# GNN layer and mixture-of-experts FFN on one core: the first value of four columns per placement tile multiplied by GpSimd instead of VectorE

## The reference

```python
def _L0_gnn_ref(x, W1, b1, W2, b2, edge_index):
    dst = edge_index[0]
    nbr = edge_index[1]
    agg = jax.ops.segment_sum(x[nbr], dst, num_segments=n)
    cnt = jax.ops.segment_sum(jnp.ones((nbr.shape[0],), x.dtype), dst, num_segments=n)
    mean = agg / jnp.maximum(cnt, 1.0)[:, None]
    return x @ W1.T + b1 + mean @ W2.T + b2
...
x = x + _L0_gnn_ref(_layernorm(x, axis=-1), ..., edge_index)
x = x + _L0_ffn_ref(_layernorm(x, axis=-1)[None], ...)[0]
```

## Time and profile before

| | us |
|---|---|
| Median of 3 runs | 1964.03 |
| Lowest and highest of them | 1962.31, 2257.03 |
| The profiled execution's own time | 1958.99 |
| Span in its trace | 1956.9 |
| Placement of the first group in it (first L1472 to last L1486 on VectorE) | 68.41 to 104.84 |
| First gather (L650) | 108.33 |

### The profile page before, as it was taken

How to read it: one execution, slowest core, us unless ns; L and a number is a source line. 1 busy time by engine, 2 the same in 40 slices (tenths; PEclk the granted TensorE clock), 3 DMA queues, 4 the chain that set the end, 5 groups by cost and what they waited for, 6 DMA issues and landing times.

```text
span 1956.9 us, 41490 instructions
## 1 busy us (share of the span) xinstructions
PE 1768.8 (90%) x11167; PEld 1495.9 (76%) x11167; DVE 967.5 (49%) x2315; ACT 1117.8 (57%) x3316; POOL 1193.3 (61%) x1141
## 2 busy tenths in 40 slices
PE   6888998899887898878877879999999999999997
PEld 4655875588555677656665768999999999999997
DVE  6868977898467787633334786311111111111111
ACT  5964875477544699755652657544444444444443
POOL 1167777788777777777777743444554454544543
PEclk9989999999999899999999989999999999999999
DMA  9333333333333333344443767724424424242421
GB/s 313 101 88 103 95 98 102 101 90 86 100 104 103 100 97 95 104 127 139 144 138 110 243 229 236 222 36 128 125 40 121 98 66 120 39 127 38 124 36 20
DMA packets 113112, 224.31 MB, mean 115 GB/s; under 512 B 27286, under 2 KB 76604, under 8 KB 107094
## 3 DMA queue, kind: packets, MB, share of 16 engines
q0 software_dynamic: 61152, 129.45, 26.7%
q1 hardware_dynamic: 32576, 74.98, 11.2%
q10 hardware_dynamic: 19254, 18.32, 3.0%
HBM read 371.77 MB, written 34.91 MB: 208 GB/s over the span
## 4 chain that ended last, share of the span: by engine, by line
PE 46%; POOL 31%; issue 11%; DMA 6%; DVE 4%; SPq 1%; ACT 1%; DVEq 0%; POOLq 0%; ACTq 0%
POOL arena L650 31%; PE bank L1315 19%; PE bank L1331 18%; DMA arena<-ytab,arena 4%; PE bank L1280 2%; PE bank L1055 2%; PE bank L1101 1%; PE bank L1303 1%; DMA gw<-in_gw2t 1%; SPq L465 1%; DVE agg L1949 1%; DMA ytab<-arena 1%; DMA agg<-in_b 0%; DMA agg<-xtab_a,arena 0%; PE bank L1255 0%
## 5 line engine op out<-in xcount | busy, mean ns | idle before, releaser
L650 POOL DMA_INDIRECT arena<-ytab,arena x784 | 800.6, 1021 | 240.1 <-issue 230.9
L1280 PE MATMUL bank<-arena 128*128 x2356 | 631.4, 395 | 111.4 <-SPq L525 109.9
L1280 PEld LDWEIGHTS bank<-arena 128*128 128x128 f32 x2356 | 415.2, 197 | 212.8 <-issue 151.7
L948 ACT ACTIVATE arena<-bank,agg 128x128 f32<-128x128 f32 x840 | 308.4, 367 | 403.7 <-PE bank L1315 345.7
L1315 PEld LDWEIGHTS bank<-arena,agg 128*128 128x128 f32 x3360 | 392.2, 193 | 5.8 <-issue 1.0
L1315 PE MATMUL bank<-arena,agg 128*128 128x128 f32 x3360 | 393.8, 276 | 0.6 <-issue 0.6
L1949 DVE TENSOR_TENSOR agg<-agg,bank 128x257 f32 x589 | 248.1, 421 | 294.1 <-PE bank L1280 254.6
L1331 PE MATMUL bank<-agg,arena 128*128 128x256 f32 x1680 | 380.1, 380 | 0.4 <-DMA agg<-in_b 0.4
L683 POOL DMA_INDIRECT out<-arena x105 | 170.8, 1627 | 324.2 <-issue 241.4
L1331 PEld LDWEIGHTS bank<-agg,arena 128*128 128x128 f32 x1680 | 311.5, 190 | 38.2 <-DMA agg<-in_b 0.7
L794 ACT ACTIVATE arena<-lanes,arena 128x128 f16<-128x128 f16 x816 | 247.9, 386 | 19.3 <-DVEq L1577 19.3
(11 more groups left out here) (275 smaller groups left out, 1661.5 us busy)
## 6 DMA issues: line engine op xcount, KB each, us to landing
agg<-in_w SPq DMA_DIRECT2D x210, 1024.0 KB
agg<-in_b SPq DMA_DIRECT2D x105, 128.0 KB
arena<-ytab,arena POOLq DMA_INDIRECT x784
ytab<-arena SPq DMA_DIRECT2D x12, 512.0 KB, 3.2
arena<-in_xt ACTq DMA_DIRECT2D x24, 256.0 KB, 3.0
node<-in_x SPq DMA_DIRECT2D x6, 896.0 KB, 12.3
agg<-in_xt SPq DMA_DIRECT2D x6, 896.0 KB, 12.9
out<-node ACTq DMA_DIRECT2D x6, 896.0 KB
```

The lines of the kernel that those rows point to most:

```text
L650: pool.indirect_dma_start(out=rows[:, v % RU, h, 0:D], out_offset=None, in_=ytab[:, :], in_offset=bass.IndirectOffsetOnAxis(ap=rowidx[g % ...
L948: act.activation(hT[:, m, :], hidden_bank(j, m)[:, 0:T], ACT.Relu, bias=b1b[:, b, m:m + 1]).then_inc(s_fr, 1)
L1280: mm = pe.matmul(bank[bank_of(n)][:, 0:W], onehot[n // QUAD % 2][:, n % QUAD, h, :], pair[:, h * W:(h + 1) * W], start=(h == 0), stop=(h = ...
```

## The change

GpSimd multiplies the four columns that L1478 multiplied, with an operation of the same shape (125 x 4 x 128, 16-bit). It waits for the tile's `ohq`, for the ring's buffer, and once for the first values. TensorE waits for it ahead of column 4 of each tile. VectorE's program loses L1478 in the 16 tiles, and has one more wait for its own pipeline, and a semaphore's increment, behind the doubling of the first values. GpSimd's last three clearings were one behind another; now the fifth comes behind tile 5, the sixth behind tile 11, and the seventh at the end.

```diff
@@ -632,8 +632,26 @@
 
             for i in range(BY_DVE):
                 means(i)
-            for i in range(NB):
+            def values_by_row(i):
+
+                j, c = i, i * PC
+                m = PC - BY_ACT
+                pool.wait_ge(s_q, j + 1)
+                if j >= PB:
+                    pool.wait_ge(s_pt, j - PB + 1)
+                pool.wait_ge(s_val1, 1)
+                pool.tensor_tensor(val[j % PB][0:EP, BY_ACT:PC, 0, :].rearrange("p u (a r) -> p u a r", r=2),
+                                   ohq[j % PB][0:EP, BY_ACT:PC].rearrange("p u (a r) -> p u a r", r=2),
+                                   val1_2[0:EP, c + BY_ACT:c + PC, :].rearrange("p (u a) r -> p u a r", a=1).to_broadcast([EP, m, P // 2, 2]),
+                                   ALU.mult).then_inc(s_vg, 1)
+
+            for i in range(NB - 3):
                 cleared(i)
+            for i in range(PT[0]):
+                values_by_row(i)
+                if i in (5, 11):
+                    cleared(NB - 3 + (5, 11).index(i))
+            cleared(NB - 1)
 
@@ -1049,6 +1067,8 @@
                 if u == 0:
                     pe.wait_ge(s_c, j + 1)
                     pe.wait_ge(s_vd, j + 1)
+                if g == 0 and u == BY_ACT:
+                    pe.wait_ge(s_vg, j + 1)
                 if g > 0 or u < BY_ACT:
                     pe.wait_ge(s_va, scaled_before(g, c) + 1)
@@ -1473,10 +1493,6 @@
                                 ALU.is_equal).then_inc(s_c, 1)
                 v.wait_ge(s_q, j + 1)
-                if s == 0:
-                    m = PC - BY_ACT
-                    v.tensor_tensor(in_pairs(val[j % PB][0:EP, BY_ACT:PC, 0, :]), in_pairs(ohq[j % PB][0:EP, BY_ACT:PC]),
-                                    pairs(val1_2[0:EP, c + BY_ACT:c + PC, :], m, P), ALU.mult)
                 n = POINTED if s == NG - 1 else 0
@@ -1625,6 +1641,8 @@
                     begun(v.tensor_copy(val1_2[0:EP], twice(val1[0:EP, :], first)))
+                    settle()
+                    v.sem_inc(s_val1)
                 if t in (2, 4, 7):
```

More of the change, by code:

```diff
@@ L417, in gnn_moe @@
         s_row = [sem(f"rows_in{r}") for r in range(RU)]
-        s_units, s_free, s_apart, s_oh16, s_oh, s_ohd, s_agg, s_sum = (sem(n) for n in ("units_in", "units_free", "lanes_apart", "onehot16_ready", "onehot_widened", "onehot_direct", "segment_multiplied", "segment_summed"))
+        s_val1, s_vg, s_units, s_free, s_apart, s_oh16, s_oh, s_ohd, s_agg, s_sum = (sem(n) for n in ("first_values_ready", "values_by_gpsimd", "units_in", "units_free", "lanes_apart", "onehot16_ready", "onehot_widened", "onehot_direct", "segment_multiplied", "segment_summed"))
         s_w1s, s_w1c, s_mm1, s_add1, s_flat, s_pre = (sem(n) for n in (
```

## The result

| | before | after | difference |
|---|---|---|---|
| Median of 7 runs each (us) | 1961.88 | 1971.96 | +10.1; ratio 1.0057 [1.0045, 1.0069] |
| The profiled execution's own time | 1958.99 | 1971.96 | +13.0 |
| Its span | 1956.9 | 1969.9 | +13.0 |
| First `ohq` to the end of the last second values on VectorE (the stage) | 36.4 | 47.2 (68.29 to 115.50) | +10.8 |
| First gather starts at | 108.33 | 118.97 | +10.6 |

What follows compares the result with a forecast made beforehand. VectorE was taken to pace the placement ahead of the first gather, whose start sets the end. Terms -5.3, 16 x 1.2 and -1.2 gave +12.7, rounded +13: 1964 + 13 = 1977 us, range 1960 to 1988.

Steps and rivals of the forecast that it cites:

- Who carries it: From the first gather on, GpSimd is issue-bound, so a delay of its start at 108.33 us delays the end equally.
- -5.3 us for L1478: In the placement stage VectorE loses 16 operations of 0.33 us, all on the path: -5.3 us.
- Exclusion: In the placement, GpSimd's reading product and VectorE's two-SBUF-input operations cannot overlap, so their times add: 3.0 us per tile, not 2.14.
- +19.2 us, 16 x 1.2: In the placement, GpSimd's product adds 1.2 us (two reads and a write) in each of 16 tiles.
- -1.2 us, one product hidden in the small steps behind tile 1: Behind tile 1, one GpSimd product runs while VectorE's chain of small steps waits for its own pipeline: -1.2 us.
- Tiles every 3 us: In the placement, a tile takes 3 x 0.60 us on VectorE plus 1.2 on GpSimd, 3.0 us instead of 2.14.
- The ring's gaps, 0 to +8: With the three-tile ring full, both engines might wait for TensorE's placing; half showing would be 16 x 0.5 = +8 us.
- Costed at nothing: TensorE's wait ahead of column 4, moved clearings, settling and later lists: no added cost, though fifth and sixth clearings might cost +1 to 3.
- Rival (a): No exclusion in the placement: GpSimd's product is hidden and TensorE becomes the pace, -3.2 us, 1961 us; chance 0.24.
- Rival (b): GpSimd paces the placement without stopping VectorE, 1.8 to 2.4 us per product: 1961 to 1971, say 1966 us; chance 0.13.
- Rival (c): GpSimd's product in the placement is far dearer, an exclusive price of 2.8 us: 2009 us; chance 0.03.

Runs made afterwards that it cites:

- without: The changed kernel with the four columns' product on no engine, TensorE reading `ohq` itself there; ratio to before 0.9981, first `ohq` to first gather 36.7 us.
- writes: The changed kernel with two GpSimd clearings per tile in place of its product, all waits kept; ratio to before 0.9986, first `ohq` to first gather 36.6 us.
- beside: VectorE keeps L1478; GpSimd multiplies constants of the same shape, awaited by nobody within the stage; ratio to before 1.0069, first `ohq` to first gather 52.8 us.
- one_input: The changed kernel with GpSimd multiplying `ohq` by 1, one input read instead of two; ratio to before 1.0017, first `ohq` to first gather 45.4 us.
- steps_later: The changed kernel with VectorE's chain of small steps behind tile 3 instead of tile 1; ratio to before 1.0014, first `ohq` to first gather 47.5 us.
- again: The changed kernel, unedited, profiled a second time on another chip; ratio to before 1.0050, first `ohq` to first gather 50.1 us.

## Why the prediction was right, step by step

- **Who carries it** (the first gather's start goes to the end): held. The stage +10.8, the first gather +10.6, the span +13.0, the medians +10.1. It is not exact. The profiled executions also differ in the gathers' own time (800.6 against 805.8 us busy): the last gather starts 16.2 us later, and 3.3 of them are made good behind it. No run was made for this part. Of the 1977 us that were forecast, 5 were not there: 3 in the difference of the medians, and 2 because the median before came out at 1961.88 instead of 1964.03.
- **-5.3 us for L1478**: held, on VectorE; `without` and `writes` took 5.0 off its stage (3.3 off the first gather's start, where TensorE is the pace).
- **Exclusion** (the term that decides): held, and `beside` shows it alone, +12.9 us with no wait, while `writes` shows that the waits and the writing cost nothing. The single row of 7 elements that the prediction went by told the truth. So did the Trainium skill (SBUF — State Buffer, section "Who interferes with whom"): products of two SBUF inputs stood for a reader (1.52 us) and not for a writer (0.678). That whoever issues first takes the pair fits the thirteen tiles; it does not fit the third, where GpSimd waited while seven later operations began.
- **+19.2 us, 16 x 1.2**: this is the mis-sized term. The price was taken as GpSimd's two reads and its write, 1.2 us; the product takes 1.03 with VectorE stopped, and only the reads exclude. Measured: 0.85 for two reads of 512, 0.43 for two of 256, 0.42 for one of 512, each time about 0.83 ns per element read, so 13 x 0.85 = 11.0 us. The prediction's own lower bound, 0.8 "if the write hides behind the reads", was the right one, and its 0.7 ns per element read was near. "Whoever has the access keeps it for a whole operation" fits VectorE's operations. Of GpSimd's it is nearly so for the product (0.85 of the 0.90 us behind `ohc`), and false in `one_input` (0.42 of 1.35).
- **-1.2 us, one product hidden in the small steps behind tile 1**: no product ran there. The second tile's product ended before them and cost its 0.85, and the third was passed over behind them. What hid three products was the stop.
- **Tiles every 3 us**: 2.65, by the same error.
- **The ring's gaps, 0 to +8**: they came, but as one stop of 5.07 us instead of a half microsecond per tile. The working had the case (GpSimd gets in only when the ring is full) and then said that the sum stays the same unless both wait for TensorE; they did, once, for 5 us, and it hid three tiles' 0.85. The exclusion cost 11.0 us where the sum had 19.2 less 1.2, and the stop of 5.1 was outside the sum: these two errors partly cancel, so +13 came out near +10.8 partly by luck.
- **Costed at nothing**: the seventh clearing had 2.38 us to spare, the fifth and the sixth cost nothing, the wait ahead of column 4 cost nothing in `writes`. Held.
- **Rival (a)**, no exclusion: its condition is false. Its size was right: -3.2 worked out, -3.3 in `without` and `writes`, with TensorE as the pace, as it said. **Rival (b)**, GpSimd as the pace: false, it waits 1.23 us for `ohq` in most later tiles. Its lower end was also mis-stated: 16 x (1.8 - 2.14) is -5.4, and -3 is the bound that TensorE sets in (a). **Rival (c)**: would need 2.8 us.

## What to carry to other kernels

Before moving a VectorE operation to GpSimd, count the elements that GpSimd will read while VectorE does operations with two SBUF inputs: here each cost VectorE 0.83 ns, so a product that VectorE did in 0.33 us cost it 0.85. Where VectorE sets the pace, as here, such a move loses however idle GpSimd is. A job in which GpSimd only wrote was free beside them. And a consumer that waits for GpSimd can stand long in a stage where VectorE never pauses: here a product was passed over until VectorE ran into its own ring, or, in `steps_later`, until VectorE came to a step with one input in SBUF. Whether such a step, put in between on purpose, would shorten the stop was not tested.

## What the runs showed of the hardware

- VectorE, in products with two SBUF inputs, stands for GpSimd's reads alone: 0.42 us per 512 16-bit elements read, even where GpSimd's operation lasts 1.86 us, and nothing beside GpSimd's clearings (678 ns with them and without).
- Which of the two is served depends on what VectorE did last: behind a step of 1 x 112, a waiting product of GpSimd was passed over by overlapping operations of VectorE (5.61 us instead of 1.41 in the changed kernel), in all of the runs in which such a step stood there and GpSimd read. Behind steps of 128 x 7 and 128 x 112 it was let in after one operation. The cause is open, and whether the single partition decides is not shown.
- On TensorE an idle time of 3.85 us was followed by a stretch at a granted clock of 0.50, in which four products took 2.02 us instead of 1.08. In `again` the same 3.85 us were followed by 1.34 us for the four, and the stop of VectorE was 4.23 us instead of 5.07.
